# Scores ahead of the projection unit, rounds without a loop, residual addition first: one decoder layer on one NeuronCore

## The reference, cut to what matters

```python
x = x + attn(layernorm(x))      # x: 16 batches x 256 tokens x 512
x = x + conv_mix(ctx, ctx, layernorm(x))
x = x + mixed_ffn(layernorm(x))

# attn: 32 query heads, 8 key/value heads (4 query heads share one), head size 64
qkv = x @ qkv_w.T + qkv_b
q, k = rope(q), rope(k)
logits = einsum(q, k) / 8, masked causal and to a window of 128
w = exp(logits - m) / (sum(exp(logits - m)) + exp(sink - m))
out = (w @ v) @ out_w.T + out_b
```

## Time and profile before

| What | Value |
| --- | --- |
| Median of three runs | 2185.22 us (2184.93 to 2189.57) |
| The profiled execution: its own time | 2187.89 us |
| Its span, first to last instruction | 2185.7 us |
| Matmuls busy (PE) | 1988.6 us, 91% of the span |
| VectorE busy (DVE) | 1610.8 us, 74% |
| ScalarE busy (ACT) | 935.4 us, 43% |
| GpSimd busy (POOL) | 771.3 us, 35% |
| Mean granted TensorE clock, as a share of full speed | 0.971 |

### The profile page before, as it was taken

How to read it: one execution, slowest core, us unless ns; L and a number is a source line. 1 busy time by engine, 2 the same in 40 slices (tenths; PEclk the granted TensorE clock), 3 DMA queues, 4 the chain that set the end, 5 groups by cost and what they waited for, 6 DMA issues and landing times. The chain is left out here.

```text
span 2185.7 us, 49034 instructions
## 1 busy us (share of the span) xinstructions
PE 1988.6 (91%) x15488; PEld 1619.9 (74%) x15488; DVE 1610.8 (74%) x5784; ACT 935.4 (43%) x3481; POOL 771.3 (35%) x879
## 2 busy tenths in 40 slices
PE   5799999999999989899999999999996899999699
PEld 4688877787877867778778777878774677677587
DVE  4777777776777766667767676767774699999787
ACT  3454545454545444444544454544542222222233
POOL 2244334333333333323322232223330454454354
PEclk8999999999999999999999999999998899999799
DMA  5147111111111121211111111111112633333364
GB/s 184 51 102 150 51 59 48 49 61 56 49 50 49 66 85 56 72 36 68 49 50 49 50 50 56 53 51 49 50 50 66 225 90 86 85 88 88 105 226 157
DMA packets 73966, 170.37 MB, mean 78 GB/s; under 512 B 6928, under 2 KB 15632, under 8 KB 73632
## 3 DMA queue, kind: packets, MB, share of 16 engines
q1 hardware_dynamic: 64160, 146.80, 20.4%
q0 software_dynamic: 3840, 8.39, 2.1%
q10 hardware_dynamic: 5760, 12.59, 1.5%
HBM read 109.03 MB, written 50.41 MB: 73 GB/s over the span
## 5 line engine op out<-in xcount | busy, mean ns | idle before, releaser
L646 ACT ACTIVATE pr<-pr,mx 128x128 f32<-128x128 f32 x1024 | 399.0, 391 | 441.5 <-DVE mx L847 441.5
L717 POOL TENSOR_TENSOR m<-m,rope_sb 128x512 f32<-128x512 f32 x160 | 206.6, 1291 | 563.2 <-ACT m L633 563.2
L514 PE MATMUL wP<-xTh,wh 128*128 128x256 f32 x1280 | 380.5, 297 | 5.8 <-DVE xTl L807 3.5
L514 PE MATMUL wP<-xTl,wh 128*128 128x256 f32 x1280 | 366.1, 286 | 0.0
L514 PE MATMUL wP<-xTh,wl 128*128 128x256 f32 x1280 | 364.7, 285 | 0.0
L1095 PE MATMUL y<-kv,tap 128*128 128x288 f32 x1280 | 330.1, 414 | 27.4 <-DVE res L1143 9.3
L1095 PEld LDWEIGHTS y<-kv,tap 128*128 128x128 f32 x1280 | 240.5, 192 | 116.9 <-issue 24.3
L856 DVE TENSOR_TENSOR den<-ac,es 128x4 f32<-128x4 f32 x256 | 63.1, 246 | 302.0 <-ACT es L649 270.5
L574 PE MATMUL oP<-woh,oTh 128*128 128x512 f32 x512 | 223.3, 436 | 55.0 <-DVE x L895 55.0
L514 PEld LDWEIGHTS wP<-xTh,wh 128*128 128x128 f32 x1280 | 248.7, 194 | 8.5 <-issue 3.1
L514 PEld LDWEIGHTS wP<-xTl,wh 128*128 128x128 f32 x1280 | 248.6, 194 | 0.0
(11 more groups left out here) (108 smaller groups left out, 3781.8 us busy)
## 6 DMA issues: line engine op xcount, KB each, us to landing
tap<-padded_taps SPq DMA_DIRECT2D x64, 256.0 KB, 3.4
kk<-in_ctxt SPq DMA_DIRECT2D x64, 192.0 KB, 3.1
x_in<-in_x SPq DMA_DIRECT2D x16, 512.0 KB, 3.7
xt_split<-xTh SPq DMA_DIRECT2D x16, 512.0 KB, 3.1
xt_split<-xTl SPq DMA_DIRECT2D x16, 512.0 KB, 4.2
xb<-in_x SPq DMA_DIRECT2D x16, 512.0 KB, 4.5
fsum<-in_factors POOLq DMA_DIRECT2D x8, 1024.0 KB, 8.6
x_part_rows<-x SPq DMA_DIRECT2D x16, 512.0 KB, 3.1
```

What stands on the lines that cost most here:

```text
L514: last = pe.matmul(wP[:, h * T:(h + 1) * T], w[:, n, c, h * P:(h + 1) * P], a[:, s, c, :], start=(c == 0 and i == 0), stop=(c == KD - 1 an ...
L646: act.activation(pr[:, s, a, cols], pr[:, s, a, cols], ACT.Exp, bias=mx[:, s, i:i + 1], scale=-1.0, accum_out=ac[:, s, i:i + 1])
L717: pool.tensor_tensor(m2[:, s], m2[:, s], rope_sb[:, 1 if i == 0 else 0, 1:3], ALU.mult).then_inc(sin_ready, 1)
```

## The change

Three edits in `attention_part`: `bodies` becomes a Python loop over all 17 rounds, so that every round stands in the program with constant wait values; on TensorE the scores go ahead of the projection unit (and of the transposes of rows) in the even slots; on VectorE the residual addition goes to the front of its slot.

```diff
-        def bodies(eng, body):
-            body(Body(0, 0, 0))
-            body(Body(1, 0, 1))
-            with eng.Fori(2, HM - 1) as m:
-                body(Body(m, 0))
-            body(Body(HM - 1, 0, HM - 1))
-            body(Body(HM, 1, HM))
-            body(Body(HM + 1, 1, HM + 1))
-            with eng.Fori(HM + 2, NM - 1) as m:
-                body(Body(m, 1))
-            body(Body(NM - 1, 1, NM - 1))
-            body(Body(NM, 1, NM))
+        def bodies(body):
+            for m in range(NM + 1):
+                body(Body(m, 0 if m < HM else 1, m))
...
                         if y.here(p, 3):
                             p_transposes(y, p, j)
+                        if j == 0 and y.here(p, 2):
+                            scores(y, p)
                         n = unit_of(p, j)
                         if n is not None and not y.drain:
                             unit(y, p, n)
...
-                        if j == 0 and y.here(p, 2):
-                            scores(y, p)
                         u, jj = (p - 4, 1) if j == 0 else (p - 3, 0)
...
+                        if residual_tile(y, p, j) is not None:
+                            residual(y, p, residual_tile(y, p, j))
                         u, jj = (p - 3, 1) if j == 0 else (p - 2, 0)
                         if y.here(u, 0):
                             divide(y, u, jj)
                         if y.here(p, 3):
                             mask_transposed(y, p, j)
-                        if residual_tile(y, p, j) is not None:
-                            residual(y, p, residual_tile(y, p, j))
```

More of the change, by code:

```diff
@@ L444, in body @@
                             sp.dma_start(xb[:], rows(x, r + 1)).then_inc(xb_landed, 16)
-            bodies(sp, body)
+            bodies(body)
             sp.wait_ge(x1t_evac, 2 * B)
@@ L600, in body @@
                             out_projection(y, p, s)
-            bodies(pe, body)
+            bodies(body)
             for t in range(NT):
@@ L694, in body @@
                             split_high(i, n)
-            bodies(act, body)
+            bodies(body)
             for t in range(NT):
@@ L769, in body @@
                         pool.tensor_tensor(tap0[:, 0:1], tap0[:, 0:1], tap0[:, 1:2], ALU.add).then_inc(tap_added, 1)
-            bodies(pool, body)
+            bodies(body)
             power(ve2, rs2, ve2_ready, rs2_ready, B)
@@ L962, in body @@
                             split_low(i, n)
-            bodies(dve, body)
+            bodies(body)
             ln2_stats(2 * B - 1, 1)
```

## The result

| | Before | Changed |
| --- | --- | --- |
| Median | 2185.07 us (4 runs, 2184.65 to 2189.57) | 2221.16 us (4 runs, 2218.56 to 2224.13) |
| Ratio to before | 1 | 1.0163, 95% interval 1.0147 to 1.0178 |
| Profiled execution, span | 2187.89, 2185.7 us | 2221.76, 2220.0 us |

A forecast was written before the change was run, and what follows sets the result against it. The prediction took a ring through VectorE and ScalarE, waiting for late units, to set the pace. New orders +64 us and loops -33 us gave +31 on 2185.22: about 2216 us, range 2188 to 2242.

The forecast's parts named there:

- The ring and its late units: VectorE/ScalarE chain from score step through exponentials, division, masked copy, evacuation; units delayed by early scores: slot 0 +1.61 us, slot 6 +1.1.
- Scores' start: On TensorE, early scores wait for the previous slot's score step, starting at the earliest 1.31 us after its mark.
- Slot 1's unit: On TensorE, this unit waits for the evacuation of slot 0's unit, about 0.9 us each time.
- Slots 2 and 4: Scores ahead of row transposes: first sweep nothing; second sweep 0.8 us gained in slot 3, about +0.45 from slot 4.
- Residual addition: At the front of VectorE's slot: slot 3 first sweep +0.2 us; slot 7 -0.25 first sweep, -0.6 second.
- Windows: Length of one window after the change: about 51.3 us in the first sweep and 50.6 us in the second.
- The deduction of 5 us for windows with split weights: Taken off 69.3 us: VectorE's extra work at the start and change of sweeps makes slot 0's late unit cost less.
- The loops: Writing out all rounds removes the stalls at eight jumps back, about 4 us each: 33 us won.
- the ring was not elastic: Rival: TensorE sets the pace and VectorE catches up in slots with slack; 2152 us, chance 0.14.
- The stall did leave with the loops: Rival denied here: the jumps' stall stays in straight code; about 2249 us, chance 0.08.
- reading of the clock: Rival: more gaps put TensorE at 1.2 GHz more often, lengthening units; only in the range's upper end, no separate chance.

## Why the prediction was right, point by point

- *The ring and its late units*: right in place and size. Slot 0 was forecast at 7.90 us and is 7.88; slot 6 at 6.64 and is 6.64. That the units cause it is shown twice: with no unit behind early scores slots 0 and 6 are back at 5.65 and 5.47 us (2122.4 us in all), and with the score step ahead of the evacuation, so that the ring no longer waits for the unit, 39 of the changed kernel's microseconds come back.
- *Scores' start*: forecast 1.31 us behind the mark, it is 1.40 in the row above by the modelled start. The sum of the slot still comes out because another term was too large by as much: from the unit's end to the evacuation it is 1.13 us (483.24 to 484.37), 1.26 were in the sum.
- *Slot 1's unit*: its wait for the evacuation was forecast at about 0.9 us and is 0.60. Nothing in the sum hangs on it; slot 1 lasts 5.65 us as before. All waits of TensorE together are about 4 us a window, where about 5 were forecast.
- *Slots 2 and 4*: in the first sweep forecast as nothing; slot 5 grew from 6.87 to 7.01 us (508.98 to 515.99), 0.14 a window. In the second sweep slot 3 is 7.62 us (it was 8.5 in looped rounds and 8.35 in straight ones), a gain of 0.7 to 0.9 as forecast; slot 5 is 7.62 instead of 6.97, +0.65 where +0.45 was forecast.
- *Residual addition*: slot 3 at 7.23 us (7.28 forecast), with the wait for GpSimd in the row. The reason given for it, that the old order hid this wait behind the division, isn't quite it: the division itself was held until the bias addition ended. Slot 7 is at 5.93 and 5.66 us (-0.3 and -0.6, forecast -0.25 and -0.6). In the whole the addition's move is worth 19 us with the scores first. What I had not seen is its other side: with the scores in their old place it makes the division collide with GpSimd's rotation, 1.2 us in slot 3, of which slot 5 gives 0.4 back. In the changed kernel the two miss each other by 0.22 us (502.21 and 502.43). The forecast didn't look at this, so the +0.2 for slot 3 held by luck.
- *Windows*: 51.28 and 50.8 us, forecast 51.3 and 50.6. The deduction of 5 us for windows with split weights was too large: windows 15 to 18 grew by 5.0 us (219.65 to 224.7) where the full price would be 8, but window 1 grew by 3.9 where it would be 2.7. That and the second sweep's slot 5 are most of the 5 us between forecast and result.
- *The loops*: -33 us forecast, -35 measured with the old orders; the two orders on top of that were forecast at +64 and are +70 (2151.62 to 2221.16). Taken the other way round the parts are about +57 for the orders with the loops kept, and -22 for the loops. The forecast could add its two parts because it priced both from straight and looped rounds of the old orders.
- *Rivals*: the ring was not elastic. Slots 0 and 6 grew by what the late units gave, and nothing of it was caught up in slots 1, 2 and 4, which have the lengths they had. The stall did leave with the loops, and the mean granted clock did not fall: 0.978 over the changed kernel, 0.971 before. The prediction's reading of the clock is not right as it stands: it says that the drops in straight rounds follow idle stretches longer than those expected (0.5 to 1.5 us), but between 81.6 and 85.0 us, in a straight round of the kernel before, the granted clock was 0.50, and TensorE's idle stretches in the 10 us ahead of it were of 1.31, 1.07 and 0.59 us.

## What to carry to other kernels

An engine that is busy 90% of the time need not set the pace: mark one instruction that comes once per step, take its distances, and look whether a chain through the slower-looking engines adds up to each distance without a gap. Before something is moved ahead of a long block, ask who waits for the end of that block: a gap in front of the moved piece costs nothing by itself, a late end of the blocks behind it does, even one slot further on. A move to the front of a queue brings its waits along for everything behind it, so ask for all of them, and give steps that differ (here slot 3 of the first sweep, slot 4 of the second) an order of their own.

## What the runs showed of the hardware

- A taken jump back of a hardware loop stops an engine for 3 to 4 us here: 4.2 us at most on VectorE, 4.0 on TensorE. Over the whole kernel eight of them cost 22 to 35 us, 2.7 to 4.4 us each, and the rounds written out showed no such stall in straight code.
- The price of one jump is 1.8 to 3.2 us where the granted clock of TensorE stays at 1.00 behind it, 3.0 to 5.2 us where it falls to 0.50 for 3.4 us, and 5.9 to 6.0 us where it does so for 6.8 us. A stretch of 3.4 us at the lower level without a jump made a window 1.6 us longer (50.08 against 48.48 us in the version with the addition first).
- VectorE's multiplication of SBUF by a column, 0.28 us a piece, can be held by a GpSimd instruction: four of them took 1.91 instead of 0.87 us beside a rotation of 1.36 us. The Trainium skill, "SBUF — State Buffer", says in its list of terms that the two engines share a pair of ports by an exclusive lock held for the whole instruction; the rows agree in that the four ended together with GpSimd's instruction, at 478.35 and 478.27, and that the division's first instruction beside the bias addition ended with that one, at 480.46 and 480.45. No run here took the rotation away by itself; with the same order on VectorE but the rotation later, the four took 0.87 us.
